# Causal attention with four heads packed per 128 rows: full-array score matmuls on zero-padded queries against row-tiled score matmuls, read out two heads at a time

## Chip, cores and metric

One NeuronCore of one Trainium2 chip runs the whole program in one launch. The metric is the device time of one execution in microseconds (us); lower is better. A time is told as the median of several executions.

## What is computed

The program is six residual stages on a stream x of 4 batches of 1024 tokens of 128 features: a mixture-of-experts FFN, a bidirectional selective scan, the same FFN again, a ternary FFN, causal attention, and the ternary FFN again. The change touches the attention stage only:

```python
B, S, E, H = (2, 256, 128, 16)        # H = 16 heads of 8; batch and length are taken from x: 4 and 1024
hsz = esz // H
qkv = x @ w_in.T + b_in
q, k, v = jnp.split(qkv, 3, axis=-1)
q, k, v = (to_heads(q), to_heads(k), to_heads(v))
scale = np.float32(1.0 / np.sqrt(hsz))
scores = jnp.einsum('bhqd,bhkd->bhqk', q * scale, k)
scores = scores + causal_bias
attn = jax.nn.softmax(scores, axis=-1)
out = jnp.einsum('bhqk,bhkd->bhqd', attn, v)
out = out @ w_out.T + b_out
...
x = x + _L1_attn_ref(_layernorm(x, axis=-1), ...)
```

## The kernel before

`attention` (from L1448) works in slots. A slot is one group of four heads of one batch: 4 groups by 4 batches are 16 slots. While a slot computes the exponentials and the output of its own group, it computes the row maxima of the group after it and the projections (queries, keys, values) of the group two ahead. A stage "pre" stands in front (projections of group 0 and 1, maxima of group 0), four slots "first", a loop of two iterations of four slots "mid" (`all_slots`, L1571), four slots "last" (its last slot has no maxima), and "tail".

A slot has twelve steps, v = 0 to 11. `STEPS` (L1475) gives for each step the chunk c of 512 queries and the tile kt of 128 keys for the exponentials: 512, 384, 256, 128 columns in steps 0 to 3 (chunk 0, all on the diagonal), then 512 five times, 384, 256, 128 (chunk 1, of which steps 8 to 11 lie on the diagonal, `DIAG`). `SU` (L1470) gives for each step the tile of queries and the chunk of keys for the maxima: 512, 384, 128, 256, 512, 512, 256, 512, 128, 384, 512, 512 columns; eight of the twelve (all but steps 4, 5, 7 and 10) lie on the diagonal.

In each step the TensorE queue holds, for each of four heads j, one score matmul for the exponentials (`exp_unit`, L1682: stationary K, moving Q, keys on the PSUM partitions) and one for the maxima (`max_unit`, L1666: stationary Q, moving K, queries on the partitions), on the diagonal with an accumulating matmul that adds the mask to its last 128 columns (L1669). Behind head j = 1 stand the value matmuls of the step before (`value_step`, L1698): four heads, each into its own 32 partitions of `PV`, each shown as two records. At the end of a step stands what else passes through the one bank `M` (`m_use`): in step 0 and 2 the queries' projection of three passes (L1654 to L1656), in 4 and 5 that of the keys, in 6 that of the values (twelve small matmuls), in 1 and 7 the transposes that bring the split maxima into the queries' rows, in 3 and 9 the transposes of the output; some slots have up to three more (xT, oT, O). Each use of `M` waits until the previous one has been read.

ScalarE reads each exponential's bank (`exp_unit`, L1771), 512 columns or fewer, into one of eight buffers `pt`; it reads the projections twice (qf L1790, qh L1793) and takes out `PV` (L1780). VectorE takes the maximum of each score bank (L1865), merges two chunks' maxima (L1871), builds the split queries and keys (`stack`, L1932), adds the maxima to the queries (L1887) and reads the rest of `M`. GpSimd splits the maxima (L2004 to L2008) and zeroes the forbidden half of the diagonal block of `pt` for the four heads of a step at once (`mask_step`, L2013 and L2016); the value matmuls of a diagonal step wait for it.

A head has 8 features, split in three parts of precision plus maxima rows, so 32 rows of the 128. The keys `K` hold four heads stacked in 128 rows. The queries `Q` are one tensor of 128 rows per head, with zeros in the other heads' 96 rows: GpSimd clears them once (L1987, L1990), VectorE builds the four heads in `stk`, and ScalarE copies 32 rows for each head into `Q` (`queries`, L1810, in steps -3, -2, 9 and 10). So each score matmul contracts all 128 rows.

The PSUM tensor `W` has six banks: three in turn for the maxima, three for the exponentials, one head each. A matmul waits for the reader of the unit three units back of its own kind.

Of the kernel before, what the change touches and what calls it, by code (L numbers as in the profile page):

```python
# [1453 lines left out]
def attention(nc, tag, x, ident, w):  # L1454
# [25 lines left out]
    SPS = NS // NT  # L1480
    DIAG = [v for v, (c, kt) in enumerate(STEPS) if kt >= TPB * c]
# [38 lines left out]
    def copies(stage, g, v):  # L1520

        uses = slot_uses(stage, g)
        use = uses.get(v - 2) if v < 0 else uses.get({9: 0, 10: 2}.get(v))
        return use if use and use[0] == "Q" else None


# [42 lines left out]

    def all_slots(slot, eng):  # L1570

        slot("pre", 0, -1)
        for g in range(GROUPS):
            slot("first", 0, g)
        with eng.Fori(1, NBATCH - 1) as i:
            for g in range(GROUPS):
                slot("mid", i, g)
        for g in range(GROUPS):
            slot("last", NBATCH - 1, g)
        slot("tail", NBATCH, 0)  # L1580

    with ExitStack() as ctx:
# [13 lines left out]
        stk = sb("stk", [P, 2, BLK])  # L1596
# [9 lines left out]
        Q, K = sb("Q", [P, GROUPS * GH, SEQ], F32R), sb("K", [P, GROUPS, SEQ], F32R)  # L1606
# [10 lines left out]
        W = ph.ps("W", [P, 6, BLK])  # L1617
# [8 lines left out]
        s_st, s_q = sem("st"), sem("q")  # L1626
# [12 lines left out]
        def tile(t):  # L1639
            return slice(t * P, (t + 1) * P)  # L1640

# [3 lines left out]
        with nc.Block() as block:  # L1645
# [6 lines left out]
            def _(pe):  # L1652
# [5 lines left out]
                def max_unit(G, g, s):  # L1658

                    t, c, j = SU[s]  # L1660
                    n = G * NS + s
                    cols = min(BLK, (t + 1) * P - c * BLK)
                    diag = c == t // TPB
                    wait(pe, s_max, n - 2)
                    out = W[:, s % 3, 0:cols]
                    mm = pe.matmul(out, Q[:, g * GH + j, tile(t)], K[:, g, c * BLK:c * BLK + cols],  # L1666
                                   start=True, stop=not diag)
# [4 lines left out]
                def exp_unit(stage, i, g, v, j):  # L1672
# [3 lines left out]
                    if kt == 0 and j == 0:  # L1676

                        pe.wait_ge(s_Md, through("D", stage, i, g, 1) if c else through("D", stage, i, g - 1, 7))
                    u = v * GH + j
                    n = (i * GROUPS + g) * NT * GH + u  # L1680
                    wait(pe, s_exp, n - 2)
                    pe.matmul(W[:, 3 + u % 3, 0:BLK - r * P], K[:, g, tile(kt)],  # L1682
                              Q[:, g * GH + j, c * BLK + r * P:(c + 1) * BLK],
                              start=True, stop=True).then_inc(s_T, 1)

                def value_step(G, g, v):
# [4 lines left out]
                    for j in range(GH):  # L1691
                        u = v * GH + j
                        n = G * NT * GH + u
                        if v in DIAG:
                            pe.wait_ge(s_pm, G * len(DIAG) + DIAG.index(v) + 1)
                        else:
                            pe.wait_ge(s_exp, n + 1)
# [37 lines left out]
                def slot(stage, i, g):  # L1735
                    G = i * GROUPS + g
                    uses = slot_uses(stage, g)
                    for v in steps(stage):
                        if v == -5:
                            pe.wait_ge(s_pre, 3)  # L1740
                        for j in range(GH):
                            if has_exp(stage):
                                exp_unit(stage, i, g, v, j)
                            if has_max(stage, g) and v >= 0:
                                if v == 0 and j == 0:
                                    pe.wait_ge(s_q, 2 * G + 4)
                                    pe.wait_ge(s_st, 4 * G + 8)
                                max_unit(G + 1, (g + 1) % GROUPS, SPS * v + j)
                            if j == 1 and v > 0 and has_exp(stage):
                                value_step(G, g, v - 1)  # L1750
                            if j == 1 and v == 0 and stage != "pre" and (stage, g) != ("first", 0):
# [7 lines left out]
            def _(act):  # L1759
# [4 lines left out]
                def exp_unit(i, g, v, j):  # L1764
                    c, kt = STEPS[v]
                    r = max(0, kt - TPB * c)
                    u = v * GH + j
                    n = (i * GROUPS + g) * NT * GH + u
                    act.wait_ge(s_T, n + 1)
                    wait(act, s_pv, n - PR + 1)  # L1770
                    act.activation(pt[:, u % PR, 0:BLK - r * P], W[:, 3 + u % 3, 0:BLK - r * P],  # L1771
                                   ACT.Exp).then_inc(s_exp, 1)
# [29 lines left out]
                def queries(i, use, j):  # L1802

                    if isinstance(i, int) and i == 0 and use[2] == 1 and j == 0:
                        act.wait_ge(s_cst, 6)
                    kind, rel, n, c = use
                    G = (i + rel) * GROUPS + n
                    if j == 0:
                        act.wait_ge(s_st, 4 * G + c + 1)
                    last = act.activation(Q[head(j), n * GH + j, chunk(c)], stk[head(j), c, :], ACT.Copy)  # L1810
                    if j == GH - 1:
                        last.then_inc(s_q, 1)

                def slot(stage, i, g):
                    for v in steps(stage):
                        if v == -5:
                            act.wait_ge(s_pre, 1)
                            act.wait_ge(s_cst, 3)
# [4 lines left out]
                        for j in range(GH):  # L1823
                            if has_exp(stage):
                                exp_unit(i, g, v, j)
                            before = use_before(stage, g, v, 1)
                            if before:
                                m_read(stage, i, before[1], before[2], before[0], j)
                            copied = copies(stage, g, v)
                            if copied:  # L1830
                                queries(i, copied, j)
# [4 lines left out]
            def _(dve):  # L1836
# [19 lines left out]
                def max_unit(G, g, s):  # L1856

                    t, c, j = SU[s]
                    n = G * NS + s
                    dve.wait_ge(s_S, n + 1)  # L1860
                    if s == 0:
# [325 lines left out]
```

## Time and profile before

| | us |
|---|---|
| median of 3 executions | 3504.2 |
| lowest, highest | 3501.76, 3508.26 |
| profiled execution, own time | 3511.2 |
| profiled execution, span from the first to the last instruction | 3509.5 |

Of the 1.7 us between the last two nothing is shown in the trace. Mean granted TensorE clock over the span: 0.941 of full speed. Busy over the whole span: TensorE 88%, VectorE 71%, ScalarE 60%, GpSimd 37%. The attention stage lies between 2393.9 and 3223.8 us of the span; its steady slots are the 694.8 us from 2473.57 to 3168.41, fifteen slots, and the sixteenth follows.

In the rows below, a number after x is a count. A line of the timeline reads: start, duration, engine, line of the kernel, operation, names and shapes, and in square brackets the idle time of the engine before it with what ended it. Matmuls are pipelined, so their durations overlap; what one costs TensorE is the distance from its start to the next start.

### The profile page before, as it was taken

Reading aid. Unit: us, or ns where it says so; the run is one execution under the profiler, and the core shown is the slowest. Engines: PE = TensorE matmul, PEld = TensorE weight load, DVE = VectorE, ACT = ScalarE, POOL = GpSimd, SP = SyncE. Lnnn points to the kernel's source line nnn. Section 1 sums busy time; section 2 is a strip of 40 time slices with the busy share of each in tenths; the row PEclk is TensorE's granted clock in tenths of the full one; section 3 lists DMA queues with packets and bytes.
Section 4 is the critical chain, followed back from the end, with each engine's and each line's share of the span. In section 5 each row is a group of like instructions: output and inputs, shape, how many; then the busy total and the mean of one; then the engine's idle time right before and its main releaser. Section 6 shows DMA issues by size and latency. Waiting matters only on the chain. (4 is left out here: it accounts for less than half of the span.)

```text
span 3509.5 us, 45842 instructions
## 1 busy us (share of the span) xinstructions
PE 3084.5 (88%) x12718; PEld 1980.3 (56%) x12718; DVE 2478.8 (71%) x4603; ACT 2116.1 (60%) x3647; POOL 1289.3 (37%) x1266
## 2 busy tenths in 40 slices
PE   6999995989989899877999997995898888986998
PEld 4767673434334333325677676773665555653786
DVE  5666665899999999996666664545887777773543
ACT  5667674665655555636666674552676766764554
POOL 2223233787878888862232230002111111111000
PEclk9999997999999999998999998996999999997999
DMA  2000001222222222211000001000000000000000
GB/s 81 1 1 1 1 0 48 64 73 65 73 70 70 72 70 70 71 59 57 1 1 0 0 0 34 1 0 10 1 1 1 1 2 1 1 1 22 12 0 24
DMA packets 55714, 93.18 MB, mean 27 GB/s; under 512 B 8060, under 2 KB 13468, under 8 KB 55300
## 3 DMA queue, kind: packets, MB, share of 16 engines
q1 hardware_dynamic: 54980, 90.15, 8.4%
q8 instruction: 84, 1.38, 0.2%
q14 instruction: 138, 1.13, 0.1%
q10 hardware_dynamic: 512, 0.53, 0.1%
HBM read 88.03 MB, written 2.62 MB: 26 GB/s over the span
## 5 line engine op out<-in xcount | busy, mean ns | idle before, releaser
L1425 POOL TENSOR_TENSOR a_hc<-a_H,a_cb 128x512 f32<-128x512 f32 x512 | 623.3, 1225 | 191.8 <-DVE a_H L1341 157.1
L481 DVE TENSOR_TENSOR m_hl<-m_raw,m_hh 128x512 fp32r<-128x512 f32 x576 | 412.5, 720 | 293.2 <-ACT m_hh L326 288.1
L1158 PE MATMUL a_Y<-a_hc,ident 128*128 128x512 f32 x1024 | 523.3, 630 | 22.7 <-POOL a_hc L1425 20.6
L321 ACT ACTIVATE m_raw<-m_U,m_b 128x512 f32<-128x512 f32 x576 | 404.9, 707 | 221.2 <-PE m_U L198 213.0
L1865 DVE TENSOR_REDUCE a_mx<-a_W 128x1 f32<-128x512 f32 (+3 forms) x768 | 396.9, 549 | 164.9 <-PE a_W L1669 104.4
L1771 ACT ACTIVATE a_pt<-a_W 128x512 f32<-128x512 f32 (+3 forms) x768 | 353.5, 492 | 233.5 <-PE a_W L1682 230.1
L1265 ACT ACTIVATE a_dA<-a_dt,a_aneg 128x512 f32<-128x512 f32 x512 | 338.7, 714 | 171.2 <-DVE a_H L1341 94.7
L1158 PEld LDWEIGHTS a_Y<-a_hc,ident 128*128 128x128 f32 x1024 | 179.6, 193 | 244.6 <-issue 127.8
L1682 PE MATMUL a_W<-a_Q,a_K 128*128 128x512 f32 (+3 forms) x768 | 305.6, 403 | 4.8 <-issue 2.7
L326 ACT ACTIVATE m_hh<-m_U,m_b 128x512 fp32r<-128x512 f32 x432 | 303.5, 702 | 0.0
L1666 PE MATMUL a_W<-a_K,a_Q 128*128 128x512 f32 (+3 forms) x768 | 275.8, 366 | 11.2 <-DVE a_mx L1865 10.9
L209 PE MATMUL m_Y<-m_hh,m_w2h 128*128 128x512 f32 x576 | 247.6, 430 | 13.1 <-DVE m_prod L451 6.3
L562 POOL TENSOR_TENSOR m_acc<-m_acc,m_prod 128x512 f32<-128x512 f32 x96 | 129.6, 1350 | 319.0 <-DVE m_prod L451 317.5
L2013 POOL TENSOR_TENSOR a_spare<-a_zero 128x1 f32<-128x1 f32 x128 | 25.9, 203 | 589.7 <-ACT a_pt L1771 589.7
L196 PE MATMUL m_U<-m_xh,m_w1h 128*128 128x512 f32 x576 | 235.3, 408 | 2.7 <-ACT m_hh L326 2.6
L210 PE MATMUL m_Y<-m_hh,m_w2l 128*128 128x512 f32 x576 | 234.9, 408 | 0.0
L212 PE MATMUL m_Y<-m_hl,m_w2h 128*128 128x512 f32 x576 | 233.7, 406 | 0.0
L1682 PEld LDWEIGHTS a_W<-a_Q,a_K 128*128 128x128 f32 x768 | 148.5, 195 | 145.3 <-issue 67.9
L862 DVE TENSOR_TENSOR t_hl<-t_raw,t_hh 128x512 fp32r<-128x512 f32 x128 | 88.1, 691 | 198.9 <-ACT t_hh L779 198.8
L198 PE MATMUL m_U<-m_xl,m_w1h 128*128 128x512 f32 x576 | 227.5, 395 | 0.0
L197 PE MATMUL m_U<-m_xh,m_w1l 128*128 128x512 f32 x576 | 227.3, 395 | 0.0
L1365 DVE TENSOR_TENSOR a_bx<-a_u,a_Bp 128x512 f32<-128x512 f32 x256 | 173.0, 676 | 64.5 <-PE a_Bp L1095 39.1
(277 smaller groups left out, 6869.3 us busy)
## 6 DMA issues: line engine op xcount, KB each, us to landing
a_cb<-a_crow SPq DMA_DIRECT2D x256, 256.0 KB, 3.1
m_wst<-moe_w SPq DMA_DIRECT2D x36, 256.0 KB, 2.6
t_wst<-ternary_w SPq DMA_DIRECT2D x22, 256.0 KB, 2.6
out<-x SPq DMA_DIRECT2D x1, 2048.0 KB, 8.7
a_hc<-mamba_conv_rows SPq DMA_DIRECT2D x1, 1024.0 KB, 6.8
a_dA<-mamba_bc_sel SPq DMA_DIRECT2D x1, 512.0 KB, 7.5
a_crow<-a_dbl ACTq DMA_DIRECT2D x16, 32.0 KB, 1.6
a_wst<-attention_w_qk SPq DMA_DIRECT2D x1, 512.0 KB, 3.4
```

What stands on the lines that cost most here:

```text
L196: pe.matmul(U[:, k, :], w1h[:, j, c], xh[:, par, :], start=True, stop=False)
L209: pe.matmul(Y[:, q, :], w2h[:, j, c], hh[:, q, k, :], start=(k == 0), stop=False)
L321: act.activation(raw[:, k, :], U[:, k, :], ACT.Silu, bias=b1[:, j, k:k + 1])\
L326: act.activation(hh[:, q, k, :], U[:, k, :], ACT.Silu, bias=b1[:, j, k:k + 1]).then_inc(s_hh, 1)
L481: dve.tensor_tensor(hl[:, q, k, :], raw[:, k, :], hh[:, q, k, :].bitcast(F32), ALU.subtract).then_inc(s_hl, 1)
L1158: pe.matmul(Y[:, h, :], ident[:], hc[:, g % HCRING, :], start=False, stop=v == NS - 1).then_inc(s_y, 1)
L1265: act.activation(dA[:, G % ARING, :], dt[:, b % 2, h, :], ACT.Exp, scale=aneg[:, d, h, v:v + 1]).then_inc(s_dA, 1)
L1425: pool.tensor_tensor(hc[:, G % HCRING, :], H[:, s, span], cb[:, v % RING, :], ALU.mult).then_inc(s_hc, 1)
L1666: mm = pe.matmul(out, Q[:, g * GH + j, tile(t)], K[:, g, c * BLK:c * BLK + cols], start=True, stop=not diag)
L1682: pe.matmul(W[:, 3 + u % 3, 0:BLK - r * P], K[:, g, tile(kt)], Q[:, g * GH + j, c * BLK + r * P:(c + 1) * BLK], start=True, stop=True).the ...
L1771: act.activation(pt[:, u % PR, 0:BLK - r * P], W[:, 3 + u % 3, 0:BLK - r * P], ACT.Exp).then_inc(s_exp, 1)
L1865: dve.tensor_reduce(dst, W[:, s % 3, 0:min(BLK, (t + 1) * P - c * BLK)], AX, ALU.max)\
```

## The change

`Q` becomes one tensor of 128 rows per group, laid out as `K` is: four heads stacked by 32 rows. `stk`, the copies into `Q` and both clearings of `Q` go. Each score matmul, of both kinds, takes one head's 32 rows of `Q` and `K` (array rows 32j to 32j+31), all 128 output partitions. The mask matmuls keep 128 rows. The addition of the maxima to the queries is one instruction on 128 rows in place of four on 32.

`W` becomes three pairs of banks, used in turn by both kinds: the sequence is exponentials pair, maxima pair, exponentials pair, and so on (`pairs`, `ring`, `three_back`). A pair holds two heads. ScalarE and VectorE read a pair in one instruction. A matmul pair waits for the reader of the pair three back in that one sequence, which is of the other kind. Semaphores are counted per pair. The value matmuls of the step before now stand behind the first exponentials pair and the first maxima pair; each two of them wait for one pair's exponentials. On ScalarE both reads of a projection now stand between the two pairs of a step.

```diff
-                def max_unit(G, g, s):
...
+                def free_pair(stage, i, slot, v, jp, kind):
+
+                    last = three_back(stage, slot, v, jp, kind)
+                    if last:
+                        of, back, n = last
+                        G = i * GROUPS + slot - back
+                        if of == "E":
+                            pe.wait_ge(s_exp, G * PS + n)
+                        else:
+                            pe.wait_ge(s_max, (G + 1) * PS + n)
+                def max_pair(stage, i, slot, g, v, jp):
...
+                    for j in (2 * jp, 2 * jp + 1):
+                        mm = pe.matmul(W[:, r, j % 2, 0:cols], Q[head(j), g, tile(t)],
+                                       K[head(j), g, c * BLK:c * BLK + cols], start=True, stop=not diag)
                     if diag:
-                        mm = pe.matmul(W[:, s % 3, cols - P:cols], idr[:], mneg[:], start=False, stop=True)
+                        for j in range(2):
+                            mm = pe.matmul(W[:, r, j, cols - P:cols], idr[:], mneg[:], start=False, stop=True)
                     mm.then_inc(s_S, 1)
...
+                def exp_pair(stage, i, g, v, jp):
...
+                    for j in (2 * jp, 2 * jp + 1):
+                        mm = pe.matmul(W[:, at, j % 2, 0:BLK - r * P], K[head(j), g, tile(kt)],
+                                       Q[head(j), g, c * BLK + r * P:(c + 1) * BLK], start=True, stop=True)
+                    mm.then_inc(s_T, 1)
...
+                    act.activation(pt[:, u % PR:u % PR + 2, 0:BLK - r * P],
+                                   W[:, ring(stage, g, v, jp, "E"), :, 0:BLK - r * P], ACT.Exp).then_inc(s_exp, 1)
...
-                    last = act.activation(Q[head(j), n * GH + j, chunk(c)], stk[head(j), c, :], ACT.Copy)
...
+                    dve.tensor_reduce(dst, W[:, ring(stage, slot, v, jp, "M"), :, 0:min(BLK, (t + 1) * P - c * BLK)],
+                                      AX, ALU.max).then_inc(s_max, 1)
...
-                        for jj in (2 * j, 2 * j + 1):
-                            q = Q[head(jj), n * GH + jj, chunk(c)]
-                            ins = dve.tensor_tensor(q, q.bitcast(F32), M[head(jj), :], ALU.add)
+                        q = Q[:, n, chunk(c)]
+                        last = dve.tensor_tensor(q, q.bitcast(F32), M[:], ALU.add)
...
-                pool.memset(Q[:, 0:GH, :].bitcast(F32), 0.0).then_inc(s_cst, 1)
                 pool.memset(V[:], 0.0).then_inc(s_cst, 1)
                 pool.memset(mt[:], 0.0).then_inc(s_cst, 1)
-                pool.memset(Q[:, GH:, :].bitcast(F32), 0.0).then_inc(s_cst, 1)
```

## Rows read from the trace of the kernel before

**Rows 1.** Stretches: length, busy us of each engine (instructions), granted clock, DMA share, GB/s.

```profile
2473.57:3168.41 694.84, 619.15 (x4022) 413.77 (x4021) 530.47 (x1078) 481.77 (x985) 123.47 (x328) 0.97 0.01 1
2944.11:2988.20 44.09, 39.64 (x267) 26.25 (x266) 34.86 (x71) 32.56 (x67) 8.16 (x22) 1.00 0.00 1
```

**Rows 2.** Groups of instructions in the attention stage: busy us, mean ns, idle before.

```profile
L1887 DVE TENSOR_TENSOR a_Q<-a_Q,a_M 32x512 fp32r<-32x512 f32 x128 | 87.2, 681 | 8.3 <-PE a_M L1720 6.5
L1810 ACT ACTIVATE a_Q<-a_stk 32x512 fp32r<-32x512 f32 x128 | 80.1, 626 | 3.8 <-DVE a_stk L1932 1.2
```

**Rows 3.** Timeline of TensorE, step 5 and the value matmuls in it.

```profile
2962.28 0.39 PE L1682 MATMUL a_W<-a_Q,a_K 128*128 128x512 f32 x1
...
2962.96 0.39 PE L1666 MATMUL a_W<-a_K,a_Q 128*128 128x512 f32 x1
2963.28 1.06 PE L1698 MATMUL a_PV<-a_pt,a_V 128*32 128x512 f32 x8
2964.27 0.50 PE L1682 MATMUL a_W<-a_Q,a_K 128*128 128x512 f32 x1
2964.61 0.39 PE L1666 MATMUL a_W<-a_K,a_Q 128*128 128x512 f32 x1
```

**Rows 4.** Timeline of TensorE in the expert FFN: one matmul of 16 rows.

```profile
503.32 0.39 PE L198 MATMUL m_U<-m_xl,m_w1h 128*128 128x512 f32 x1
503.63 0.50 PE L232 MATMUL m_R<-m_wts,m_sel 16*128 16x512 f32 x1
504.06 0.50 PE L209 MATMUL m_Y<-m_hh,m_w2h 128*128 128x512 f32 x1
504.40 0.40 PE L210 MATMUL m_Y<-m_hh,m_w2l 128*128 128x512 f32 x1
```

**Rows 5.** Timeline of all engines, readers of 512 columns in a run.

```profile
2835.35 2.48 DVE L1865 TENSOR_REDUCE a_mx<-a_W 128x1 f32<-128x512 f32 x4 [0.57 <-PE a_W L1666]
2810.90 1.08 ACT L1771 ACTIVATE a_pt<-a_W 128x512 f32<-128x512 f32 x2 [1.44 <-PE a_W L1682]
```

**Rows 6.** Timeline of all engines, step 11: copies, the mask step, the value matmuls behind.

```profile
2985.38 0.38 ACT L1771 ACTIVATE a_pt<-a_W 128x256 f32<-128x256 f32 x1
2985.79 0.62 ACT L1810 ACTIVATE a_Q<-a_stk 32x512 fp32r<-32x512 f32 x1
2985.84 0.19 POOL L2013 TENSOR_TENSOR a_spare<-a_zero 128x1 f32<-128x1 f32 x1 [3.30 <-ACT a_pt L1771]
2985.98 0.63 POOL L2016 TENSOR_SCALAR_AFFINE_SELECT a_pt<-a_pt 128x512 f32<-128x512 f32 x1
2986.67 0.64 PE L1698 MATMUL a_PV<-a_pt,a_V 128*32 128x256 f32 x8 [1.24 <-POOL a_pt L2016]
```

**Rows 7.** Timeline of all engines, step 2: the maxima added, the next use of M.

```profile
2952.20 1.36 DVE L1887 TENSOR_TENSOR a_Q<-a_Q,a_M 32x512 fp32r<-32x512 f32 x2
2953.90 1.39 DVE L1887 TENSOR_TENSOR a_Q<-a_Q,a_M 32x512 fp32r<-32x512 f32 x2
2955.34 0.50 PE L1654 MATMUL a_M<-a_xh,a_wh 128*128 128x512 f32 x1 [1.04 <-DVE a_Q L1887]
```

**Rows 8.** Timeline of GpSimd, VectorE and TensorE at the start of the stage.

```profile
2404.44 0.95 POOL L1989 MEMSET a_mt<- 128x1024 f32 x1
2405.33 10.48 POOL L1990 MEMSET a_Q<- 128x12288 f32 x1
2398.70 6.77 DVE L1850 CAST a_idr<-ident 128x128 fp32r<-128x128 f32 x1
2406.80 10.68 DVE L1937 TENSOR_SCALAR a_xn<-x,a_mv,a_rstd 128x128 f32<-128x128 f32 x8
2431.24 0.77 PE L1654 MATMUL a_M<-a_xh,a_wh 128*128 128x512 f32 x1 [3.46 <-ACT a_qh L1793]
```

**Rows 9.** Waits of TensorE, 2473.57 to 3168.41: who for whom, us in total, times, longest.

```profile
PE a_PV L1698 <- POOL a_pt L2016: 31.9, 36, 1.2
PE a_M L1654 <- DVE a_Q L1887: 16.6, 14, 2.1
```

More of the change, by code:

```diff
@@ L1519, in attention @@
             for st, gs in SLOTS.items()}
[L1520 to L1524, printed above, removed]
     WEIGHT = {"M": lambda k: 1, "D": lambda k: k not in ("Q", "K", "oT"), "A": lambda k: k in ("Q", "K", "oT"),
@@ L1568, in has_max, with pairs, slot_before, three_back @@
         return stage != "tail" and not (stage == "last" and g + 1 == GROUPS)
+    def pairs(stage, g):
+        one = [("E",)] * has_exp(stage) + [("M",)] * has_max(stage, g)
+        return [kind for _ in range(PS) for kind, in one]
+    def slot_before(stage, g):
+        if stage == "first" and g == 0:
+            return "pre", -1
+        return (stage, g - 1) if g > 0 else ("mid", GROUPS - 1)
+    def three_back(stage, g, v, jp, kind):
+        seq = pairs(stage, g)
+        at = [q for q, k in enumerate(seq) if k == kind][2 * v + jp]
+        back, q = 0, at - 3
+        if q < 0:
+            if stage == "pre":
+                return None
+            seq, back = pairs(*slot_before(stage, g)), 1
+            q += len(seq)
+        return seq[q], back, seq[:q + 1].count(seq[q])
     def all_slots(slot, eng):
@@ L1640, in tile, with ring @@
             return slice(t * P, (t + 1) * P)
+        def ring(stage, g, v, jp, kind):
+            seq = pairs(stage, g)
+            return [q for q, k in enumerate(seq) if k == kind][2 * v + jp] % 3
         def head(j):
@@ L1662, in max_unit @@
+                def max_pair(stage, i, slot, g, v, jp):
+                    t, c, _ = SU[SPS * v]
                     cols = min(BLK, (t + 1) * P - c * BLK)
                     diag = c == t // TPB
[L1664 to L1667, printed above, removed]
+                    r = ring(stage, slot, v, jp, "M")
+                    free_pair(stage, i, slot, v, jp, "M")
+                    for j in (2 * jp, 2 * jp + 1):
+                        mm = pe.matmul(W[:, r, j % 2, 0:cols], Q[head(j), g, tile(t)],
+                                       K[head(j), g, c * BLK:c * BLK + cols], start=True, stop=not diag)
@@ L1678, in exp_unit @@
                         pe.wait_ge(s_Md, through("D", stage, i, g, 1) if c else through("D", stage, i, g - 1, 7))
[L1679 to L1684, printed above, removed]
+                    at = ring(stage, g, v, jp, "E")
@@ L1822, in slot @@
                             take_out(stage, i, g, 1)
-                        for j in range(GH):
+                        for jp in range(GH // 2):
                             if has_exp(stage):
-                                exp_unit(i, g, v, j)
+                                exp_pair(stage, i, g, v, jp)
                             before = use_before(stage, g, v, 1)
                             if before:
[L1828 to L1831, printed above, removed]
+                                m_read(stage, i, before[1], before[2], before[0], 2 * jp)
+                                m_read(stage, i, before[1], before[2], before[0], 2 * jp + 1)
                 all_slots(slot, act)
```

97 lines of the change are left out of this document (37 added, 60 removed).

## The prediction

> **What bounds the kernel now.** I read the stretches first, to see where the stage's time lies. The fifteen steady slots take 694.84 us, 46.3 us each, with TensorE busy 619 us of them (89%), VectorE 530, ScalarE 482 [rows 1]. TensorE is the engine that is nearly full, and it executes in order, so the slot is its work plus its waits. For the rest I take one slot with none of the extra uses of M, at full clock: 44.09 us [rows 1]. Next the timeline of TensorE, for what each instruction costs from start to start: a score matmul of 512 columns 0.23 us (three of them lie between 2962.28 and 2962.96), the value matmuls of four heads 0.99 us from their first start to the next matmul's start, 0.10 us more ahead of them (2962.96 to 2963.28 is 0.32) and 0.11 more after them (2964.27 to 2964.61 is 0.34) [rows 3]. 0.23 us is 512 columns at 2.4 GHz (0.213) and 0.017. By columns that gives 0.18 for 384, 0.12 for 256, and I take 0.11 for 128 with its mask or weight load beside it.
>
> Summed over the slot: 96 score matmuls of 36,864 columns are 15.4 + 1.6 = 17.0 us; 32 masks at some 0.085, 2.7; weight loads that come late behind masks 1.6 (both small, estimated from the pitch of a narrow matmul); value matmuls 9.4 (six steps of 1.0, two each of 0.78, 0.57, 0.36) and 2.5 around them; uses of M 5.5 (four projections of three 512-column passes at 0.69, the values 1.33, four transposes at 0.35). That is 38.7 us. The waits of TensorE in the slot sum to 4.4 us: 1.24 for the mask step at step 11 [rows 6], 1.04 for the maxima added at step 2 [rows 7], and four of 0.2 to 0.75. Over all steady slots the list of waits has these two kinds on top, 31.9 us in 36 waits and 16.6 in 14 [rows 9]. 44.09 less 4.4 is 39.7, so the sum holds within 1 us.
>
> **The change, part by part.**
>
> *Score matmuls on 32 rows.* Two heads of a pair lie on different array rows and write different banks. Whether they run at once isn't shown for rows. For columns it is: the eight records of the four heads' value matmuls end 1.06 us after they start [rows 3], while four heads one after another, at four times 512/2.4 GHz each, would take 3.4. I take that the pair overlaps: 0.23 us for 512 columns, 0.22 for fewer (two weight loads at 0.11). The other bound is no overlap, below as a rival. 24 pairs of 512 and 24 narrower ones are 5.5 + 5.3 = 10.8 us in place of 17.0.
>
> The Trainium skill (TensorE: Matmul & The Clock Gate, Part 3: Packing small matmuls) gives row tiles that start about 4 ns apart and 3.07 times the speed for four of them; by it a pair would cost as I took it. No row here shows row tiles side by side.
>
> *Changes of the array's tiling.* Only the value matmuls leave the full array now. A matmul of 16 rows among full ones shows what rows cost: from 503.32 to 504.40 three matmuls take 1.08 us in place of 0.69, 0.39 for going there and back [rows 4]; for the 32-column tiling it is 0.10 + 0.11 [rows 3]. A change costs 0.10 to 0.195, and I take 0.17 (0.12 into the value matmuls), nearer to the row case. After the change a diagonal step goes rows, full (masks), columns (values), rows, full (masks, M), rows: five changes in each of eight steps; steps 4, 5 and 7 have four, step 10 two: 54 in a slot, 24 now. That is 9.2 us.
>
> TensorE's work after: 10.8 + 9.2, masks 3.5 (32 at 0.11), values 9.4, M 5.5: 38.4 us. So what the overlap gives, the changes of tiling take, and the work stays. The waits decide.
>
> *Readers in pairs.* VectorE's four reads of 512 take 2.48 us, a pitch of 0.60, of which 0.53 is 512 elements at one per 1.04 ns; ScalarE's two take 1.08 [rows 5]. A pair is then about 1.13 us of pitch (1.2 of duration) on VectorE and 0.92 (1.03) on ScalarE. Saved: 48 times 0.07 = 3 us and about as much of ScalarE per slot, off the path. The price is latency: a pair's exponentials end 0.40 (matmul) + 0.04 + 1.03 after its start, against about 1.0 now, and the mask step adds 0.9 from the exponentials' end to the value matmuls (2985.76 to 2986.67) [rows 6].
>
> *Copies and additions removed.* ScalarE loses 128 copies of 626 ns, 80.1 us; VectorE's 128 additions of 681 ns become 32, 65 us less [rows 2]. In a slot ScalarE's copies sit between the exponentials of steps 9 and 10 and make the mask steps late [rows 6], and the additions hold M from step 2's projection [rows 7]. Most of the slot's 4.4 us of waits comes from these two and goes. VectorE's load falls from 34.9 us [rows 1] to about 29, ScalarE's from 32.6 to about 24: neither binds.
>
> *The slot after.* I go from the second exponentials pair of one step to that of the next. The value matmuls start when both are done: TensorE's order (exponentials pair, maxima pair, masks, M, the next step's two pairs, changes of tiling), and the chain (2.37 us for a diagonal 512: 0.40 + 0.04 + 1.03 + 0.9; for others 1.53, the release of the pair, plus the next maxima pair, since that pair now waits for the exponentials three back). Then the value matmuls with their changes, 1.29, 1.07, 0.86 or 0.65 us. Step 0: order 0.23 + 0.61 + 0.69 + 0.17 + 0.22 + 0.61 = 2.53 against 2.37, so 2.53 + 1.29 = 3.83 by unrounded terms. Step 10: order 1.28, chain 0.28 + 0.04 + 0.60 + 0.9 = 1.82, plus 0.86 = 2.68. Steps 4 and 5 carry new waits: the keys' projection waits for the read of the output (1.25 in), then ScalarE takes both reads of the projection before the second pair (4 ends at 3.86, 5 at 4.04). All twelve: 3.83, 3.37, 3.38, 2.45, 3.86, 4.04, 4.09, 3.43, 3.66, 3.17, 2.68, 2.49, together 40.4 us; 2.7 of it waits. Against 44.1 that is 3.6 less. Six extra uses of M in four slots pay two changes each, 0.39 x 6/4 = 0.6. So 3.0 per slot, 45 us in fifteen. The last slot, without maxima, I put 1 us longer (its non-diagonal steps 1.53 + 1.29 = 2.8 in place of 2.65).
>
> *Start of the stage.* The normalization (eight instructions) ends 1.7 us after GpSimd's clearing of Q (2405.33 + 10.48) though it starts at 2406.80, and the cast of 128 columns lasts until the clearing of mt ends [rows 8]. So VectorE waited for GpSimd. Without 3.5 and 10.5 us of clearing, mt ends at about 2402, the normalization 3.2 us later: 12.3 us earlier. The keys' projection waited 3.46 us for a ScalarE read held behind a copy [rows 8]; 2.5 us of such waits go. The first maxima are bound by VectorE: 24 pairs and one addition in place of four save some 4 us. Together 18.8.
>
> The Trainium skill (SBUF — State Buffer, SBUF: two separate sides) states that one pair of ports is locked between VectorE and GpSimd for a whole instruction; the trace agrees, with 10.68 us for eight instructions that otherwise take 1.7.
>
> **Sum.** 45 + 18.8 - 1 = 63. From the profiled execution's 3511.2 that gives 3448; the median of the three runs is 7.0 lower, so 3441.
>
> **Rivals.**
> *The pairs don't overlap, the change doesn't do what it says.* Then 24 x 0.23 + 8 x 0.13 = 6.6 us more work per slot. 2.7 us of waits could hide some, but the exponentials start later too; I count 5. 3441 + 75 = 3516, slower. For it: no row tiles side by side in any row, and two weight loads for each pair. Against it: the column tiles do overlap. It decides from 4.2 us per slot.
> *A change of tiling costs more.* 54 changes, break-even at 63/15/54 = 0.08 above my 0.17. Leaving the 16-row matmul shows 0.20 and then 0.11 [rows 4]; if TensorE has to run empty at each change (0.39 of duration against 0.23 of pitch, 0.16 [rows 3]) and then load weights uncovered, each costs such 0.31 and a slot takes 54 x 0.14 = 7.6 us more: 3441 + 113 = 3554. Against: entering costs 0.08 there. The Trainium skill (TensorEngine Tiling (Array Packing), Tiling Modes) says that changing the tiling mode drains the engine, which is this mechanism and speaks against the change; the two visits in the trace, at 0.39 and 0.21 for two changes, agree only in part.
> *Changes at the low bound.* At 0.10 to 0.11, 3.2 us per slot less work, of which some 2 are not covered by the chain: 3441 - 30 = 3411.
> *The clock.* The steady slots have 0.97 [rows 1]. If with fewer rows in use the engine were granted 1.2 GHz, the 30 us of streaming of a slot would double: over 3850. The value matmuls use 32 columns at full clock now, which speaks against it.
>
> **Chances.** Forecast with its near bounds, 3395 to 3480: 0.60. Low bound of the changes: 0.12. No overlap: 0.15. Dear changes: 0.10. Clock: 0.03. A measurement of this kernel tells about 0.2% from no change, 7 us. Faster gets the first two and a little of partly overlapped pairs, 0.75; same, 3497 to 3511, 0.06 from between the cases; slower 0.19. The range goes from 3395, below the low case by what my waits may be too large, to 3505, where partial overlap or changes at 0.25 would lie; the upper rivals stay out.
>
> **What would show it.** Right: start to start within a pair of 512 near zero, the next pair 0.23 later; three matmuls around a mask 0.35 to 0.4 longer; normalization done near 2405; no wait for additions of the maxima; slots of 43 us; new waits of TensorE for ScalarE's release at the maxima pair. Wrong: 0.23 within a pair; changes over 0.25; VectorE or ScalarE without gaps; a granted clock under 0.95 in the steady slots.

## The result, and the profile after

The changed kernel takes 3758.65 us (median of six runs, 3739.54 to 3763.14), the kernel before beside it 3505.23 (3501.76 to 3508.26): a ratio of 1.0708, 95% interval 1.0689 to 1.0726. The forecast was 3441 with a range of 3395 to 3505. The profiled execution, the fastest of the six, took 3739.54 us, its span is 3737.8, against 3511.2 and 3509.5.

First the clock, on the page of the kernel after: the TensorE clock granted in 40 equal slices of the span, in tenths.

```profile
PEclk9999988899989999999999899755555555555999
```

From the 27th slice to the 37th, where the attention stage lies, it reads 5, which is 1.2 GHz in place of 2.4. The stretches (columns as in [rows 1]): the start of the stage, the fifteen steady slots, most of the last slot.

```profile
2418.00:2459.00 41.00, 36.21 (x123) 23.96 (x123) 25.64 (x35) 8.55 (x12) 3.01 (x4) 0.50 0.00 0
2459.10:3393.00 933.90, 915.05 (x4019) 455.55 (x4018) 445.56 (x627) 385.05 (x513) 117.70 (x328) 0.53 0.00 1
3392.00:3437.00 45.00, 33.05 (x178) 11.05 (x174) 4.01 (x9) 20.55 (x28) 7.62 (x21) 0.61 0.00 1
```

The fifteen slots take 933.9 us, 62.3 each, at a granted clock of 0.53; before they took 694.84 at 0.97 [rows 1]. These 239.1 us are more than the whole difference of the two profiled executions, 228.3: the way to the first exponentials became 14.5 us shorter (2459.1 against 2473.57), the last slot 3.9 longer. TensorE is busy 98% of the slots, so the time is its work at half the clock. VectorE's and ScalarE's loads fell, to 29.7 and 25.7 us a slot; the forecast was 29 and 24.

TensorE's timeline in two steps of a slot at 1.2 GHz (columns as in [rows 3]):

```profile
2807.47 1.94 PE L1730 MATMUL a_PV<-a_pt,a_V 128*32 128x512 f32 x8
2809.33 0.79 PE L1715 MATMUL a_W<-a_Q,a_K 32*128 32x512 f32 x2
2809.92 0.62 PE L1698 MATMUL a_W<-a_K,a_Q 32*128 32x512 f32 x2
2810.48 1.11 PE L1752 MATMUL a_M<-ident,a_mt 128*128 128x128 f32 x4
```

Two score matmuls of 512 columns are recorded together, and the next pair starts 0.59 us later. At 1.2 GHz one of them alone streams for 0.43. So the two overlap, and what this pair, which stands behind a change of tiling, costs beyond streaming is 0.16. The readers of a pair, VectorE and ScalarE (groups of instructions: line, engine, operation, count | busy us, mean ns | idle before):

```profile
L1881 DVE TENSOR_REDUCE a_mx<-a_W 128x2 f32<-128x1024 f32 (+3 forms) x384 | 367.1, 958 | 499.8 <-PE a_W L1702 364.9 <-PE a_W L1698 131.1 <-issue 3.2
L1802 ACT ACTIVATE a_pt<-a_W 128x1024 f32<-128x1024 f32 (+3 forms) x384 | 309.8, 811 | 583.1 <-PE a_W L1715 582.9
```

Both are idle for longer than they work, and what ends it is a score matmul: they wait for TensorE. The start of the stage answers to [rows 8]:

```profile
2398.53 0.95 POOL L1998 MEMSET a_mt<- 128x1024 f32 x1
2400.90 2.13 DVE L1946 TENSOR_SCALAR a_xn<-x,a_mv,a_rstd 128x128 f32<-128x128 f32 x8
```

The eight normalizations last 2.13 us where they lasted 10.68, and end at 2403.0 in place of 2417.5. The largest kind of wait of TensorE's matmuls in the steady slots sums to 7.4 us; the two kinds of [rows 9] are gone.

### The profile page after: what moved, and what is told of

It is laid out like the page before. It is cut to its first block and busy times, and to the rows that moved or that the text cites. A ratio compares the mean times of both kernels' runs of the same rounds, so it can differ in the third digit from the quotient of the medians.

```text
span 3737.8 us, 43535 instructions
## 1 busy us (share of the span) xinstructions
PE 3382.9 (91%) x12718; PEld 2015.7 (54%) x12718; DVE 2375.9 (64%) x4123; ACT 2009.1 (54%) x3135; POOL 1271.1 (34%) x1264
## 5 line engine op out<-in xcount | busy, mean ns | idle before, releaser
L1881 DVE TENSOR_REDUCE a_mx<-a_W 128x2 f32<-128x1024 f32 (+3 forms) x384 | 367.1, 958 | 499.8 <-PE a_W L1702 364.9
L1802 ACT ACTIVATE a_pt<-a_W 128x1024 f32<-128x1024 f32 (+3 forms) x384 | 309.8, 811 | 583.1 <-PE a_W L1715 582.9
L1730 PE MATMUL a_PV<-a_pt,a_V 128*32 128x512 f32 (+3 forms) x1536 | 283.0, 821 | 10.8 <-POOL a_pt L2024 8.9
L1715 PEld LDWEIGHTS a_W<-a_Q,a_K 32*128 32x128 f32 x768 | 101.4, 273 | 293.0 <-DVE a_mx L1881 176.7
L1715 PE MATMUL a_W<-a_Q,a_K 32*128 32x512 f32 (+3 forms) x768 | 244.3, 659 | 0.8 <-issue 0.8
```

The source lines that it names most:

```text
L1715: mm = pe.matmul(W[:, at, j % 2, 0:BLK - r * P], K[head(j), g, tile(kt)], Q[head(j), g, c * BLK + r * P:(c + 1) * BLK], start=True, stop=True)
L1730: pe.matmul(PV[head(j), r * P:], V[:, kt, g * GH + j, :], pt[:, u % PR, 0:BLK - r * P], start=kt == 0, stop=kt == TPB * (c + 1) - 1).then_ ...
L1802: act.activation(pt[:, u % PR:u % PR + 2, 0:BLK - r * P], W[:, ring(stage, g, v, jp, "E"), :, 0:BLK - r * P], ACT.Exp).then_inc(s_exp, 1)
L1881: dve.tensor_reduce(dst, W[:, ring(stage, slot, v, jp, "M"), :, 0:min(BLK, (t + 1) * P - c * BLK)], AX, ALU.max).then_inc(s_max, 1)
```

## Experiments

Theory 1 (of the first kernels and of those that keep the whole array) was that score matmuls on few rows of the array cause the low clock; its rival, theory 2, that the pairs do (new waits, bursts). For each kernel I give the stretch from the first exponentials' matmul to the last maxima's, fifteen slots, with the columns of [rows 1]. A time is a median; the ratio is against the kernel before, run beside it (3502 to 3506 us).

**Rows without pairs.** The kernel before, both score matmuls on their head's 32 rows, nothing else:

```diff
-mm = pe.matmul(out, Q[:, g * GH + j, tile(t)], K[:, g, ...],
+mm = pe.matmul(out, Q[head(j), g * GH + j, tile(t)], K[head(j), g, ...],
-pe.matmul(W[:, 3 + u % 3, ...], K[:, g, tile(kt)], Q[:, g * GH + j, ...],
+pe.matmul(W[:, 3 + u % 3, ...], K[head(j), g, tile(kt)], Q[head(j), g * GH + j, ...],
```

> The kernel before with one edit: each score matmul takes only the 32 rows of its head from the zero-padded queries and from the keys. Single banks, copies, additions and clearings stay as before. Theory 1 (array rows: with score matmuls on 32 rows TensorE is granted 1.2 GHz for the whole stage): granted clock in the steady slots 0.50 to 0.60 against 0.97, a slot 58 to 65 us against 46.3, time 3690 to 3800. Theory 2 (pairs: the wait for the pair three back and the late value matmuls leave TensorE waiting, and that takes the clock): clock 0.95 or more, time within 3440 to 3560.

4035.62 us, ratio 1.151 (1.148 to 1.155).

```profile
2482.50:3680.50 1198.00, 1197.11 (x4020) 609.22 (x4019) 549.19 (x1076) 505.58 (x985) 117.96 (x328) 0.50 0.00 1
```

The clock falls without a pair in the kernel. The slot takes 79.9 us, where I expected 58 to 65: single heads stream 36,864 columns where pairs stream half, which at 1.2 GHz is 15 us more than the 62.3 of after (an estimate).

**Pairs without row tiles.** The kernel after, with score matmuls that contract all 128 packed rows:

```diff
-pe.matmul(W[:, r, j % 2, 0:cols], Q[head(j), g, tile(t)], K[head(j), g, ...]
+pe.matmul(W[:, r, j % 2, 0:cols], Q[:, g, tile(t)], K[:, g, ...]
```

(and the same for the exponentials).

> The changed kernel with one edit: each score matmul takes all 128 rows of packed queries and keys, so that a score is the sum over four heads (the per-head separation is left out); pairs, order, readers and waits are those of the changed kernel, and two matmuls of a pair can no longer overlap. Theory 1: clock back to 0.93 or more, a slot 42 to 47 us, time 3430 to 3510. Theory 2: clock stays at 0.50 to 0.60, time 3700 or more.

3447.7 us, ratio 0.984 (0.980 to 0.987).

```profile
2455.10:3106.80 651.70, 614.28 (x4021) 405.87 (x4022) 446.03 (x627) 379.49 (x513) 118.60 (x329) 0.99 0.00 1
```

Full clock, 43.4 us a slot. Theory 2 falls.

**Pairs on the other heads' rows.** The kernel after, with the maxima pair taking the two heads that the exponentials pair beside it doesn't, so that all four row groups can run at once; then the same crossing in the single-head kernel with 32 rows. The lines are those of `max_pair` on TensorE and on VectorE.

```diff
-for j in (2 * jp, 2 * jp + 1):
+for j in (2 - 2 * jp, 3 - 2 * jp):
-js = slice(2 * jp, 2 * jp + 2)
+js = slice(2 - 2 * jp, 4 - 2 * jp)
```

> The changed kernel, with the maxima pair behind an exponentials pair taking the other two heads, so that four neighbouring score matmuls lie on four different groups of 32 rows. Theory 1, if what counts is the rows in use at a time: clock rises to 0.8 to 1.0 and the time falls under 3600; if what counts is the rows of each matmul by itself: clock 0.50 to 0.60, and only the overlap of two pairs is gained, some 0.2 us of 0.6 in each of 24 places of a slot, time 3670 to 3740. Theory 2: as the changed kernel, within 1% of 3758.

> The first of these kernels (single banks, 32 rows) with the maxima of heads 2, 3, 0, 1 behind the exponentials of heads 0, 1, 2, 3, so that neighbouring matmuls lie on different rows and can overlap. Theory 1 with rows in use at a time: clock 0.8 to 1.0, time under 3560; with the rows of each matmul: clock 0.50 to 0.60, time 3600 to 3720 (less than the first kernel by the overlap). Theory 2: clock 0.95 or more, time 3400 to 3500.

3512.59 us, 1.002 (1.000 to 1.004), and 3756.97 us, 1.072 (1.068 to 1.076). Crossed pairs (the rows are of the fastest of seven executions, 3485.43 us), then crossed single heads:

```profile
2458.00:3139.60 681.60, 617.19 (x4019) 302.06 (x4018) 446.12 (x627) 378.92 (x513) 119.78 (x328) 0.83 0.00 1
```

```profile
2489.60:3400.10 910.50, 888.36 (x4020) 424.54 (x4019) 543.54 (x1076) 497.16 (x985) 117.78 (x328) 0.63 0.00 1
```

With two row groups more in use at once the clock rises from 0.53 to 0.83, in the single-head kernel from 0.50 to 0.63, which lies between the 0.50 to 0.60 and the 0.8 to 1.0 that I had allowed. In the timeline of the crossed pairs, exponentials and maxima start together:

```profile
2621.66 0.44 PE L1715 MATMUL a_W<-a_Q,a_K 32*128 32x384 f32 x2
2621.66 0.44 PE L1698 MATMUL a_W<-a_K,a_Q 32*128 32x384 f32 x2
2622.04 0.44 PE L1702 MATMUL a_W<-a_mneg,a_idr 128*128 128x128 f32 x2
2622.31 0.62 PE L1752 MATMUL a_M<-ident,a_ov 128*128 128x128 f32 x4
2622.87 0.38 PE L1715 MATMUL a_W<-a_Q,a_K 32*128 32x256 f32 x2
```

It is also the place to read a change of tiling at full clock: 0.38 from rows to the full array for 384 columns that stream in 0.16, and 0.56 for four transposes on the way back to rows, which among full matmuls take 0.41 in the full-row kernel. So 0.22 for two changes with their weight loads, the one in front of the pairs (behind the value matmuls) and the one behind them, and 0.15; I had taken 0.17 for each.

**One kind of score matmul on rows.** The kernel before with only the exponentials', then only the maxima's score matmuls on 32 rows (one half of the first diff each).

> The kernel before, only the score matmuls of the exponentials on their head's 32 rows; those of the maxima keep 128. Rows in use over time decide (theory 1, after the first four runs): between the kernel before (clock 0.97 in the steady slots) and the one with both kinds on 32 rows (0.50, 79.8 us a slot); I expect 0.55 to 0.85 and 3600 to 3900 us. A rival, that any use of row tiling at all takes the clock: 0.50 and the slot over 70 us.

> The other half: only the score matmuls of the maxima on 32 rows (with the mask matmuls behind each, on 128). Theory 1: as the run before, within 100 us of it, since both kinds stream the same columns. Rival (the changes of tiling, of which this form has as many, lower the clock by themselves): 0.50 in both.

4212.35 us, 1.201 (1.199 to 1.204), and 4274.37 us, 1.219 (1.217 to 1.221).

```profile
2473.60:3859.50 1385.90, 1384.06 (x4021) 691.54 (x4020) 563.26 (x1078) 517.67 (x985) 118.07 (x329) 0.50 0.00 1
```

```profile
2493.50:3932.90 1439.40, 1438.38 (x4020) 705.41 (x4020) 562.07 (x1076) 517.97 (x985) 118.00 (x328) 0.50 0.00 1
```

Both are slower than with all of them on rows, at the same 0.50, which was the rival's forecast and not mine (0.55 to 0.85). Half of the score matmuls use the whole array and the clock doesn't rise. These kernels change tiling at every score matmul; in the timeline of the first one a 512-column matmul takes 0.72 us to the next start, 0.43 of it streaming. Either such changes keep the clock low, or rows do and I had the wrong measure of them. The next kernels part the two.

**Same rows for both, and no masks.** The kernel after with both matmuls of a pair on the same 64 rows (`half(jp)`, rows 64 jp to 64 jp + 63, in place of `head(j)`), and the kernel after without the mask matmuls (`diag = False` in `max_pair`).

> The kernel after with both score matmuls of a pair on the same 64 rows (left out: the separation of the two heads, whose scores are summed). The changes of tiling stand where they stand after; a pair no longer overlaps. Theory A (few array rows in use over time lower the clock): twice the rows of each score matmul, so the clock rises a little, to 0.5 to 0.7; slots of 55 to 70 us. Theory C (the changes of tiling, at which TensorE runs empty, lower it): the clock stays at 0.50 to 0.53, slots of 65 to 72 us. Both allow 0.5; a clock over 0.9 would speak for A alone.

> The kernel after without the 32 mask matmuls of a slot on the maxima (left out: the mask on the scores of the maxima). Two changes of tiling go at each diagonal step, 16 of 54 in a slot, and the 128-row work gets less still. Theory A (few array rows in use): the clock stays at 0.50 to 0.53, slots of 54 to 57 us from the work that is gone. Theory C (changes of tiling): the clock rises clearly, over 0.6, slots under 50 us.

4003.43 us, 1.143 (1.138 to 1.147), and 3601.25 us, 1.028 (1.021 to 1.035).

```profile
2466.20:3647.00 1180.80, 1168.47 (x4021) 669.65 (x4020) 445.74 (x627) 386.83 (x513) 116.86 (x329) 0.51 0.00 1
```

```profile
2452.60:3245.00 792.40, 737.51 (x3542) 320.99 (x3542) 449.10 (x627) 382.57 (x513) 116.83 (x328) 0.58 0.00 1
```

64 rows in every score matmul, one after another, give no more than two heads' 32 rows at once, which is 64 rows too: 0.51 and 0.53 (78.7 us a slot, over the 55 to 72 of both theories). Without masks it is 0.58, just above what the rows theory allowed and under the other's; it settles nothing: without a mask between them a maxima pair may also overlap the next exponentials pair on the other rows, and how much of the 0.05 comes from that isn't shown.

**Changes of tiling with full rows, few rows without them.** The full-row kernel with its masks on 32 rows, and with its score matmuls on rows 0 to 71.

```diff
-mm = pe.matmul(W[:, r, j, cols - P:cols], idr[:], mneg[:], ...)
+mm = pe.matmul(W[:, r, j, cols - P:cols], idr[head(j), :], mneg[head(j), :], ...)
```

```diff
-pe.matmul(W[:, r, j % 2, 0:cols], Q[:, g, tile(t)], K[:, g, ...]
+pe.matmul(W[:, r, j % 2, 0:cols], Q[0:72, g, tile(t)], K[0:72, g, ...]
```

> The full-row kernel (score matmuls on 128 rows, scores of four heads summed) with its mask matmuls on 32 rows (left out: the separation of heads, and three quarters of the mask). The changes of tiling are back around every mask, as after, while the rows in use are nearly all as in the full-row kernel. Theory A: clock 0.9 or more, slots of 46 to 50 us (43.4 and 16 to 32 changes at 0.17 to 0.2). Theory C: clock 0.5 to 0.6, slots of 60 us or more.

> The full-row kernel with its score matmuls on rows 0 to 71 (left out: the separation of heads and the part of the product from rows 72 up). No change of tiling is added to those of the full-row kernel, but only 72 rows are in use in the score matmuls. Theory A: the granted clock of the steady slots falls from 0.99 to 0.6 to 0.9. Theory C: it stays at 0.97 to 0.99 and a slot takes 43 to 44 us.

3465.11 us, 0.989 (0.986 to 0.992), and 3495.27 us, 1.000 (0.993 to 1.006).

```profile
2455.60:3122.50 666.90, 639.74 (x4022) 383.87 (x4020) 440.95 (x627) 380.90 (x513) 119.08 (x329) 0.98 0.00 1
```

```profile
2462.30:3140.50 678.20, 644.47 (x4023) 425.28 (x4023) 444.35 (x627) 380.19 (x513) 118.39 (x330) 0.94 0.00 1
```

The changes of tiling of after, among full-row score matmuls, leave the clock at 0.98 (and cost 1.0 us a slot; two masks on different rows now run side by side, which gives part of it back). 72 rows lower it a little, to 0.94, between the forecasts of the two theories. So changes alone don't cause the low clock, but neither did 72 rows, where 64 did.

**64 against 65 rows, and both halves at once.** The same edit with rows 0 to 63 and 0 to 64; and the kernel after with the two matmuls of a pair on the two 64-row halves (`half(j % 2)`).

> The full-row kernel with its score matmuls on rows 0 to 63, one row less than the next kernel (left out: the separation of heads and the part of the product from rows 64 up). Theory R (the rows that carry data count): clock and time near those of 72 rows, where the clock was 0.94, so 0.85 to 0.93 and slots of 45 to 50 us. Theory T (the size of the row tile counts: 64 rows make a tile of half the array, 65 or more one of the whole): as with the two alternating 64-row halves, clock 0.50 and a slot of 70 to 76 us.

> The same with rows 0 to 64 (left out: the separation of heads and the product from row 65 up). Theory R: as with 64 rows, clock 0.85 to 0.93. Theory T: as with 72 rows, clock 0.92 to 0.99, slots of 43.5 to 45.5 us.

> The kernel after with the two score matmuls of a pair on the two 64-row halves of the array (left out: the separation of two heads, whose scores are summed). A pair can overlap, and then the whole array is in use; the changes of tiling are those of after, 54 in a slot. Theory T in its form of shares (the part of the array in the running tiles, over time): clock over 0.9, slots of 42 to 46 us, total 3440 to 3500. If instead every matmul on less than the whole array lowers the clock whatever runs beside it: 0.50 to 0.55, slots of 62 us as after.

4015.73 us, 1.146 (1.143 to 1.149); two runs of 3576 and 3663 us (the rows are of the longer); 3453.03 us, 0.986 (0.983 to 0.988).

```profile
2468.00:3664.30 1196.30, 1185.57 (x4019) 683.62 (x4018) 445.67 (x626) 386.59 (x513) 116.58 (x330) 0.50 0.00 1
```

```profile
2461.00:3309.10 848.10, 825.34 (x4020) 545.75 (x4021) 445.45 (x627) 382.73 (x513) 118.18 (x330) 0.70 0.00 1
2461.00:2700.00 239.00, 230.19 (x1465) 152.65 (x1466) 161.69 (x226) 142.38 (x193) 44.78 (x124) 0.96 0.00 1
3000.00:3100.00 100.00, 100.00 (x379) 66.58 (x379) 40.09 (x56) 38.26 (x51) 10.37 (x29) 0.50 0.00 1
```

```profile
2461.40:3107.50 646.10, 587.31 (x4020) 304.20 (x4020) 444.11 (x627) 378.49 (x513) 118.48 (x328) 0.94 0.00 1
```

64 rows: 0.50 throughout. 65 rows: 0.96 over the first 239 us, then 0.50 to 0.64 in every 100 us, and two executions of the same kernel lie 87 us apart. The shorter of them, 3576 us, is still above all four of the 72-row kernel (3484 to 3519). So neither theory holds as I wrote it: the tile alone would make 65 rows as good as 72, and rows counted smoothly would put 64 near 65. The two halves at once have the 54 changes of tiling of after, and the clock is 0.94: what runs beside a row tile counts.

The Trainium skill (TensorEngine Tiling (Array Packing), When to Use Tiling) puts row tiling at contractions of up to 64 rows; a tile boundary between 64 and 65 is thus expected, and the two kernels differ there in changes of tiling too.

**Rows and changes together.** The 72-row kernel with masks on 32 rows, and the 64-row kernel with masks on the same 64 rows (fewer changes).

> The kernel with score matmuls on rows 0 to 71, now with its mask matmuls on 32 rows (left out: the separation of heads, the product from row 72 up, three quarters of the mask). The 54 changes of tiling of after in a slot in place of 24. With 128 rows the same edit left the clock at 0.98; with 72 rows and 24 changes it was 0.94. Theory I (rows in use and changes of tiling add up): the clock falls clearly below 0.94, to 0.5 to 0.8, slots over 50 us. Theory J (the rows or the tile alone decide): 0.90 to 0.95, slots of 45.5 to 48 us.

> The kernel with score matmuls on rows 0 to 63, now with its mask matmuls on rows 0 to 63 too (left out: the separation of heads, the product from row 64 up, half of the mask). The array's rows are retiled 16 times less around masks, 38 changes in place of 54. Theory I (rows and changes add up; 65 rows with 24 changes gave 0.70 over the stage): the clock rises to 0.55 to 0.8, slots under 70 us. Theory J (a tile of 64 rows alone decides): 0.50 as with full masks, slots of 74 to 78 us.

3816.80 us (two runs, 3795 and 3838; the rows are of the longer), 1.090 (1.075 to 1.105), and 3960.64 us, 1.131 (1.128 to 1.134).

```profile
2462.00:3487.80 1025.80, 1009.86 (x4020) 603.84 (x4018) 444.92 (x627) 386.06 (x513) 118.78 (x330) 0.56 0.00 1
```

```profile
2462.40:3607.80 1145.40, 1133.48 (x4022) 695.05 (x4021) 446.20 (x627) 386.96 (x513) 117.17 (x330) 0.50 0.00 1
```

Masks on 32 rows left the clock of the 128-row kernel at 0.98 and take the 72-row kernel from 0.94 to 0.56. Rows in use and changes of tiling act together. With that the kernels with one kind of score matmul on rows need be no contradiction, though no run separates the two in them: they have more rows in use than the 72-row kernel on average, (32 + 128)/2 = 80, and a change at every score matmul. At 64 rows fewer changes don't help: still 0.50.

**Versions that keep the whole array.** Pairs and padding can be had together. First the kernel after with the padded queries, copies and additions of before:

> The changed kernel's pairs (three bank pairs, readers for two heads, values behind the first pairs) with the zero-padded queries, copies and four additions of before, all score matmuls on 128 rows; GpSimd's clearing moved behind the normalization. Theory 1: clock 0.93 or more, a slot 43.4 us (the full-row run) plus the waits for copies and additions, 44 to 46.5; time 3465 to 3510. Theory 2 (pairs take the clock): under 0.7 and over 3700.

3523.54 us, 1.005 (1.003 to 1.007).

```profile
2458.70:3176.60 717.90, 641.66 (x4022) 424.48 (x4022) 506.47 (x717) 450.62 (x625) 119.62 (x329) 0.95 0.00 1
```

The clock is kept, but the slot takes 47.9 us (44 to 46.5 expected). TensorE's wait for the additions, the second of [rows 9], is back and longer:

```profile
PE a_M L1683 <- DVE a_Q L1929: 26.4, 14, 1.9
```

Then with the queries packed, so that one addition does for four heads, and the keys padded instead, which nothing is added to later; ScalarE copies them in steps 7 to 10 and GpSimd clears behind the normalization:

```diff
+last = act.activation(K[head(j), n * GH + j, chunk(c)], stk[head(j), c, :], ACT.Copy)
-Q[head(j), g, tile(t)], K[head(j), g, ...]
+Q[:, g, tile(t)], K[:, g * GH + j, ...]
+pool.wait_ge(s_xn, 1)
+pool.memset(K[:, 0:GH, :].bitcast(F32), 0.0).then_inc(s_cst, 1)
```

> A version meant to keep both: pairs as changed, queries packed (one addition, no copies of them), and the keys zero-padded per head in their place, copied by ScalarE in steps 7 to 10, so that every score matmul has 128 rows; clearing behind the normalization. Theory 1: clock 0.95 or more, slot 43.4 to 44.5 us, time 3440 to 3470, faster than before by 1% to 1.8%. If the copies delay the mask steps as they did in the kernel before: 3480 to 3500. Theory 2: over 3700.

> The kernel with packed queries and padded keys (3451.6 us) without the 32 mask matmuls of a slot on the maxima (left out: the mask on the scores of the maxima). All score matmuls are on 128 rows. All theories: clock 0.97 or more. TensorE loses 32 masks at some 0.11 us and part of the weight loads behind them, 3.5 to 5 us of a slot in 43.6; with the waits for the pairs' readers that become visible, 40 to 41.5 us a slot: 3400 to 3425 us.

3451.57 us (3450.01 to 3456.20), 0.985 (0.983 to 0.986), and the same without mask matmuls on the maxima 3443.25 us (3441.50 to 3445.00), 0.983 (0.980 to 0.986).

```profile
2453.40:3107.70 654.30, 616.76 (x4021) 405.97 (x4022) 446.44 (x627) 450.85 (x625) 117.78 (x329) 0.98 0.00 1
```

```profile
2453.90:3101.40 647.50, 580.66 (x3541) 340.65 (x3542) 443.38 (x628) 450.51 (x625) 121.55 (x329) 0.98 0.00 1
```

TensorE's wait for the mask step, with masks and then without:

```profile
PE a_PV L1741 <- POOL a_pt L2060: 2.7, 14, 0.3
```

```profile
PE a_PV L1741 <- POOL a_pt L2060: 16.9, 44, 1.0
```

The padded keys beat both kernels: 43.6 us a slot at 0.98, though ScalarE copies as much as before (the 128 copies are still 80.2 us). Leaving out the masks takes 36 us of work from TensorE (616.8 to 580.7 busy) and only 6.8 us from the slots; I had expected 27 to 52 in all. TensorE idles 29.3 us more (66.8 against 37.5); 14.2 of them are waits for the mask step, most of the rest short waits for readers. So at this point the chains through the other engines, that of the diagonal step first, bound the slot beside TensorE's work.

## Why the prediction was wrong

*The clock: the step that failed.* It stood among the rivals, "over 3850" at 0.03, and was set aside with "The value matmuls use 32 columns at full clock now, which speaks against it". That row shows four column tiles side by side, so the whole array runs; it says nothing of a stream that leaves half of it empty. The crossed pairs and the two halves show that this makes the difference here: 0.53 with two heads' rows, 0.83 and 0.94 when other rows run beside them. It isn't the rows alone, as the 72-row kernels show (0.94, and 0.56 with more changes of tiling). The price was too high: 19 us a slot, where I took 30. An estimate with the prediction's own terms: what grows with the clock is 26 (pairs 7.7 by their columns, values 9.4, masks 3.5, uses of M 5.5); at 0.53 that is 23 more; if the rest doesn't grow and the 2.7 us of waits vanish under the slower work, 43.3 + 23 - 2.7 = 63.6, measured 62.3. In the traces, by the distance from start to start, waits included, the slots of after differ from those of the two-halves kernel, which has the same order, in the values (16.8 us against 9.9), the score matmuls (22.5 against 17.0), the uses of M (13.1 against 8.2) and the masks (9.8 against 7.9). The chance was the fault more than the price. A stage in which TensorE is the bound depends on its clock entirely; a change that alters what share of the array works should have had a tenth or two of the chances, and the range should have reached it.

The Trainium skill (TensorE: Matmul & The Clock Gate, What's actually happening) ties the low clock to an idle engine and says that activity releases it. By that, 98% busy would mean 2.4 GHz. The trace of after disagrees: 0.53 at 98% busy. From the two-halves kernel, at 0.94 with the same changes of tiling, it differs in that half of the rows are empty.

*Overlap of the pairs: right.* They overlap, and 0.23 us for a pair of 512 columns is right too. The two-halves kernel shows it at full clock. In the first two rows an exponentials pair stands behind a change of tiling; in the last three the maxima pair stands between two pairs on the same rows, with no change before or behind it:

```profile
2480.58 0.50 PE L1718 MATMUL a_W<-a_Q,a_K 64*128 64x512 f32 x2
2480.92 0.40 PE L1701 MATMUL a_W<-a_K,a_Q 64*128 64x512 f32 x2
```

```profile
2581.50 0.39 PE L1718 MATMUL a_W<-a_Q,a_K 64*128 64x256 f32 x2
2581.72 0.40 PE L1701 MATMUL a_W<-a_K,a_Q 64*128 64x512 f32 x2
2581.95 0.23 PE L1718 MATMUL a_W<-a_Q,a_K 64*128 64x128 f32 x2
```

0.34 behind the change, 0.23 without one. The 0.11 between them belongs to the change: a single matmul behind the value matmuls shows the same 0.34 in the kernel before [rows 3]. So 0.59 at 1.2 GHz, 0.16 beyond streaming, is a pair with such a change in front, and not the price of every pair.

*Changes of tiling: right.* At full clock 0.22 for two and 0.15 for one around the mask, where I took 0.17 for each; at 1.2 GHz 0.29 for one (0.72 - 0.43, exponentials on rows). The rival of 0.31 each is out at full clock. The sum of 9.2 us takes 0.17 for all 54; with the 0.12 that the prediction names for the twelve into the value matmuls it would be 8.6.

*Waits and readers: right.* The two kinds of waits went, and both readers have slack; a read of a full pair takes 1.22 us on VectorE and 1.03 on ScalarE (1.2 and 1.03 forecast).

*The start: right at full clock, short at the low one.* In after the first exponentials start 14.5 us earlier, but 2.4 of that is because the whole stage began earlier (mt cleared at 2399.5 against 2405.4, 3.5 of it the shorter clearing): 12.1 against the 18.8 forecast, at a clock of 0.50. The normalization alone gave these 12. The full-row kernel, in which the stage began 0.3 us later than before, has its first exponentials at 2455.1, 18.5 us earlier. The last slot of after is 3.9 us longer, 1 expected, at a clock of 0.61.

*The sum at full clock: right.* With the clock nearly kept and the changes of tiling of after, the two-halves kernel takes 43.1 us a slot and 3453 us, full rows 43.4 and 3448. The sum said 43.3 (46.3 - 3.0) and 3441. TensorE's work in a slot of the two halves is 39.2 us (587.31 / 15) against 38.4 forecast, and it idles 3.9 against 2.7. "What the overlap gives, the changes of tiling take" holds between these two kernels: from start to start, waits included, the two halves take 4.4 us a slot less in the score matmuls (17.0 against 21.4) and 4.1 more in masks, values and uses of M. No run has pairs on 2 x 32 rows at full clock throughout.

## What to carry to other kernels

Before a change makes matmuls smaller in a stage that TensorE bounds, ask what share of the array is in use over time, and price the stage at both levels of the clock; a padded contraction may be the cheaper one. If row tiles are wanted, give neighbours in the queue different rows (0.53 became 0.83) and have few changes of tiling between them. Pad the operand that isn't touched again: zeros on the keys cost copies that ScalarE hides, on the queries also additions that TensorE waits for. The two padded kernels differ by 63.6 us in their slots; 33 of them are waits for additions, and TensorE is busy 25 us longer, at 0.95 in place of 0.98. Their copies also stand in different steps, and that was not tried by itself.

## What was unexpected in the hardware

- A TensorE that is 98% busy and more is granted 0.50 to 0.53 when its score matmuls use 32 or 64 rows with nothing beside them, and 0.50 also when only one kind of them is on 32 rows and the other on 128. It is granted 0.94 to 0.99 with both halves, 72 rows (with few changes of tiling), or 128. Zeros in 96 of 128 rows of an operand don't matter: 0.97 before, 0.98 with padded keys.
- With 72 rows, more changes of tiling take the clock from 0.94 to 0.56; with 128 rows it stays at 0.98. With 65 rows it was 0.96 over the first 239 us, then 0.50 to 0.64, and the two executions differ by 87 us. What exactly is weighed isn't settled by these runs.
- Two row tiles start together, and from a pair of 512 columns it is 0.23 us to the next pair on the same rows at 2.4 GHz, 0.34 where the pair stands behind a change of tiling (0.59 at 1.2 GHz). Exponentials and maxima on different rows start in the same instant.
